# A ConvLSTM and bottleneck kernel: h stored and loaded in 128 lanes where it lay in 96

## The reference, cut to what matters

```
xr = transpose(x, (2, 0, 1, 3))                       # rows first
hs_f = scan(xr, w_f, b_f, reverse=False)              # h of 48 channels, a row at a time
hs_b = scan(xr, w_b, b_b, reverse=True)
feats = concatenate([hs_f, hs_b], axis=2)             # 96 channels
y = einsum('oc,bchw->bohw', w_proj, feats)            # 48 channels
y = gamma * normalised(y) + beta;  x1 = relu(y) + x
```

## Time and profile before

| | |
|---|---|
| median of 3 runs | 1834.93 us (1831.94 to 1840.61) |
| the profiled execution | 1834.02 us |
| its span, from the first to the last instruction | 1832.2 us |
| mean granted TensorE clock | 0.953 |
| busy share: PE, weight load, DVE, ACT, POOL | 90%, 67%, 77%, 70%, 3% |
| the DMA queue of SP, share of the 16 engines over the span | 40.1% |
| HBM read and written | 98.71 and 61.49 MB |

### The profile page before, as it was taken

How to read it: one execution, slowest core, us unless ns; L and a number is a source line. 1 busy time by engine, 2 the same in 40 slices (tenths; PEclk the granted TensorE clock), 3 DMA queues, 4 the chain that set the end, 5 groups by cost and what they waited for, 6 DMA issues and landing times. The chain is left out here.

```text
span 1832.2 us, 43864 instructions
## 1 busy us (share of the span) xinstructions
PE 1646.6 (90%) x16562; PEld 1236.4 (67%) x16562; DVE 1402.7 (77%) x2264; ACT 1276.9 (70%) x2347; POOL 57.9 (3%) x88
## 2 busy tenths in 40 slices
PE   5999999999999999999996662449999999999996
PEld 5999999999999999999994220137333333333332
DVE  4777777777777777777775447643999999999996
ACT  4888888888888888888885445401666666666663
POOL 2000000000000000000000000001000000000000
PEclk9999999999999999999998996655999999999998
DMA  4555455554555555455555998892122222222223
GB/s 118 137 138 143 131 146 136 141 140 132 144 135 145 137 136 143 133 147 136 139 143 125 246 246 164 203 306 67 23 44 44 47 47 49 46 44 45 44 44 50
DMA packets 82905, 219.04 MB, mean 120 GB/s; under 512 B 20792, under 2 KB 26828, under 8 KB 82380
## 3 DMA queue, kind: packets, MB, share of 16 engines
q1 hardware_dynamic: 74504, 193.89, 40.1%
q0 software_dynamic: 6144, 16.52, 6.3%
q10 hardware_dynamic: 2180, 7.57, 2.0%
HBM read 98.71 MB, written 61.49 MB: 87 GB/s over the span
## 5 line engine op out<-in xcount | busy, mean ns | idle before, releaser
L264 PE MATMUL gates<-state,w_high 64*128 64x384 f32 x4608 | 504.9, 337 | 0.0
L1374 DVE SCALAR_TENSOR_TENSOR acc<-h1d,wt,acc 128x768 f32<-128x768 f32 x480 | 483.3, 1017 | 25.0 <-ACT acc L1285 11.8
L264 PEld LDWEIGHTS gates<-state,w_high 64*128 64x128 f32 x4608 | 416.9, 185 | 0.0
L1152 PE MATMUL psd<-h1p,wt 64*64 64x384 f32 x3456 | 300.9, 487 | 11.3 <-ACT h2p L1317 11.3
L264 PE MATMUL gates<-state,w_low 64*128 64x384 f32 x2304 | 267.6, 337 | 0.0
L264 PE MATMUL gates<-x_both,w_high 64*128 64x384 f32 x2304 | 237.4, 338 | 18.8 <-DVE w_low L380 18.8
L1152 PEld LDWEIGHTS psd<-h1p,wt 64*64 64x64 f32 x3456 | 126.2, 132 | 186.8 <-issue 172.7
L264 PEld LDWEIGHTS gates<-x_both,w_high 64*128 64x128 f32 x2304 | 207.5, 186 | 18.7 <-issue 18.7
L317 ACT ACTIVATE sig_f<-gates 48x384 f32<-48x384 f32 x384 | 187.3, 488 | 37.2 <-PE gates L264 32.3
L264 PEld LDWEIGHTS gates<-state,w_low 64*128 64x128 f32 x2304 | 208.8, 185 | 0.0
L411 DVE TENSOR_TENSOR h_new<-sig_o,tanh_c 128x384 f32<-128x384 f32 x192 | 107.2, 558 | 122.3 <-ACT tanh_c L335 122.3
(11 more groups left out here) (141 smaller groups left out, 1619.5 us busy)
## 6 DMA issues: line engine op xcount, KB each, us to landing
x_taps<-x_both SPq DMA_DIRECT2D x192, 195.5 KB, 3.1
x_raw<-x_steps SPq DMA_DIRECT2D x192, 192.0 KB, 3.2
h_rows<-h_new SPq DMA_DIRECT2D x192, 144.0 KB, 2.3
h_in<-h_rows SPq DMA_DIRECT2D x48, 576.0 KB, 7.7
x_last<-x_both SPq DMA_DIRECT2D x192, 98.0 KB, 2.9
out<-y SPq DMA_DIRECT2D x4, 4032.0 KB, 37.6
out<-z POOLq DMA_DIRECT2D x48, 336.0 KB, 5.0
sig_o<-x_steps SPq DMA_DIRECT2D x190, 48.0 KB, 2.0
```

Of the source, the lines that this page charges most:

```text
L264: return nc.tensor.matmul(gates[p][d][:, m, 0:NH], w[own, n, m, :], moving[own], start=start, stop=stop)
L1152: mm = nc.tensor.matmul(psd[64 * m:64 * m + 64, i, 0:NH], wt[own, to:to + 64], h1[own, dy + 4 * m:dy + 4 * m + 4, dx:dx + W], start=(tap = ...
L1374: nc.vector.scalar_tensor_tensor(a, window(h1d[d % 2], tap), par(D_UNITS[s], TAP + tap), a, ALU.mult, ALU.add).then_inc(acc_done if tap == ...
```

## The change

`h_rows` gets all 128 lanes. A store copies the 64 lanes of a direction, with the 16 lanes of x beside the 48 of h. A load brings 128 lanes. In the projection the weights come in one DMA with 128 lanes, those of the lanes with x being zeros; no lane is left without data, so the five memsets, their semaphore and the waits for it are gone.

```diff
             def store_h(i, e):
                 for d in range(2):
                     two = i if d == 0 else i * -1 + (H // 2 - 1)
-                    sp.dma_start(h_rows[two, HC * d:HC * d + HC, e if d == 0 else 1 - e],
-                                 h_new[e][HI * d:HI * d + HC]).then_inc(h_stored[e], 16)
+                    own = slice(HI * d, HI * d + HI)
+                    sp.dma_start(h_rows[two, own, e if d == 0 else 1 - e], h_new[e][own]).then_inc(h_stored[e], 16)
...
-        wp_loaded, gaps_zero = sem("wp_loaded"), sem("gaps_zero")
+        wp_loaded = sem("wp_loaded")
...
-            sp.wait_ge(gaps_zero, 1)
-            for d in range(2):
-                sp.dma_start(wp[HC * d:HC * d + HC], w_proj[HI * d:HI * d + HC]).then_inc(wp_loaded, 16)
-
-            def body(i, first):
+            sp.dma_start(wp[:], w_proj).then_inc(wp_loaded, 16)
+
+            def body(i):
                 for n in range(BUFS):
-                    if first:
-
-                        sp.wait_ge(gaps_zero, n + 2)
                     r = TURN * i + ROWS * n

                     at_least(sp, row_summed, r - TURN + ROWS)
-                    sp.dma_start(h_in[n][0:2 * HC], h_rows[BUFS * i + n]).then_inc(h_loaded[n], 16)
+                    sp.dma_start(h_in[n][:], h_rows[BUFS * i + n]).then_inc(h_loaded[n], 16)
...
-            pe.wait_ge(wp_loaded, 32)
+            pe.wait_ge(wp_loaded, 16)
...
-            nc.vector.memset(wp[96:128], 0.0).then_inc(gaps_zero, 1)
-            for n in range(BUFS):
-                nc.vector.memset(h_in[n][96:128], 0.0).then_inc(gaps_zero, 1)
...
-    h_rows = nc.dram_tensor("h_rows", [H // 2, 2 * HC, 2, B, W], F32).ap()
+    h_rows = nc.dram_tensor("h_rows", [H // 2, P, 2, B, W], F32).ap()
```

More of the change, by code:

```diff
@@ L459, in _ @@
         def _(sp):
-            sp.wait_ge(gaps_zero, 1)
-            for d in range(2):
-                sp.dma_start(wp[HC * d:HC * d + HC], w_proj[HI * d:HI * d + HC]).then_inc(wp_loaded, 16)
-            def body(i, first):
+            sp.dma_start(wp[:], w_proj).then_inc(wp_loaded, 16)
+            def body(i):
                 for n in range(BUFS):
-                    if first:
-                        sp.wait_ge(gaps_zero, n + 2)
                     r = TURN * i + ROWS * n
                     at_least(sp, row_summed, r - TURN + ROWS)
-                    sp.dma_start(h_in[n][0:2 * HC], h_rows[BUFS * i + n]).then_inc(h_loaded[n], 16)
-            body(0, True)
+                    sp.dma_start(h_in[n][:], h_rows[BUFS * i + n]).then_inc(h_loaded[n], 16)
+            body(0)
             with sp.Fori(1, H // TURN) as i:
-                body(i, False)
+                body(i)
         @block.tensor
         def _(pe):
-            pe.wait_ge(wp_loaded, 32)
+            pe.wait_ge(wp_loaded, 16)
             def body(i, first):
```

## The result

The kernel after takes 1816.39 us (median, 1814.15 to 1818.11) beside 1834.41 us for the kernel before, a ratio of 0.990 with a 95% interval of 0.988 to 0.9925. That is 18.0 us less; the forecast was 15.8 us less, 1818.2 us. The profiled execution took 1815.6 us, its span 1813.8.

What follows compares the result with a forecast made beforehand. The prediction took DMA loads to bound the projection and PE the recurrence; -14.7 - 1.3 + 0.2 = -15.8 us from 1834.0 gave 1818.2 us, with a range of 1806 to 1834 us.

Steps and rivals of the forecast that it cites:

- The bound: Projection: one h_in transfer paces each pair of rows, 48 x 2.38 = 114 us; the recurrence is paced by PE.
- T: Projection: time of one pair's h_in load, 2.377 us a pair before, forecast 2.07 us with 128 lanes.
- Part 1: Projection loads: 128 lanes for 96, 786,432 bytes at 380 GB/s, 2.07 us a pair for 2.377: -14.7 us.
- my trend: Projection loads: packets shorten as lanes are added, 0.0365 us for 16 more, so 0.2585 us at 128 lanes.
- rival of the same pace per byte: Projection loads: a packet keeps its 0.398 us, 3.18 us a pair, slower at 1871.4 us; chance 0.11.
- rival of lanes 0 to 63: Projection loads: the first 64 lanes set the pace, 2.38 us a pair stays, 1832.9 us; chance 0.14.
- 408.7 GB/s of a stream of loads: Projection loads: a skill page's rate for 1 MiB transfers, an estimated 1.92 us a pair, stage some 22 us shorter.
- Part 2: Projection start: one wp load and no memset before the first h_in load, so it goes out earlier: -1.3 us.
- Part 3: Recurrence stores with 64 lanes for 48: recurrence at 0, share 0.52 to 0.56, last store's landing +0.2 us.

Runs made afterwards that it cites:

- the repeat: The kernel after itself, unchanged, timed and profiled once more beside two other kernels on one chip: 1814.54 us, ratio 0.991 to the kernel before.

## Why the prediction was right, point by point

- **The bound.** Right: the projection is bound by the DMA engines before and after, and its time is about T times 48. (I read 9 and 8 in slices 22 and 23 of the DMA row; it has 9 and 9.)
- **Part 1, T = 2.07 us and -14.7 us.** The sign holds, and that the loads pace the stage. The size was 3.8 us short in the first execution (18.5 us, 0.39 us off each of 47 periods) and 1.2 us short in the repeat (15.9 us). By the windows T is 2.00 us where I said 2.07. The step that does not hold is the path to T. I read a smooth trend, a packet that gets shorter as lanes are added, through 48, 96 and 112 lanes. There is none. The table has the loads of the same stage; its last column is the median time of a 6144-byte packet in the traces' packet records, 1010 to 1050 us:

| lanes | packets per engine | GB/s | T, us | median packet, us |
|---|---|---|---|---|
| 0 to 63 | 4 | 207 | 1.90 | 0.479 |
| 0 to 95 | 6 | 246 | 2.40 | 0.401 |
| 16 to 111 | 6 | 245 | 2.41 | 0.409 |
| 0 to 111 | 7 | 263 | 2.62 | 0.378 |
| 0 to 63 and 64 to 127 | 4 + 4 | 224 | 3.51 | 0.451 |
| 0 to 127 | 8 | 394 | 2.00 | 0.234 |
| 0, 2 ... 126 and 1, 3 ... 127 | 4 + 4 | 382 | 2.06 | 0.234 |
| 0, 2 ... 126 and 1, 5 ... 125 | 4 + 2 | 339 | 1.74 | 0.234 |

 With lanes spread over all 128 the packet takes 0.234 us, however many packets a load has, and 8 of them make the 1.87 us of most pairs; with other lanes it takes 0.38 to 0.48 us. The row of 112 lanes that carried my trend (333 GB/s) was a store with rows of 36,864 bytes; the load of 112 lanes makes 263. With its 0.374 us a packet the same working would have given 0.357 us at 128 lanes, T = 2.86 us, and a slower kernel. That my T is near the measured one is luck: the trend through the wrong row happened to point at the step between 112 and 128.
- **The rival of the same pace per byte** (0.398 us a packet, T = 3.18). By the rates it is near for 96 and 112 lanes (0.400 and 0.374 us) and fails at 128 (0.250 us).
- **The rival of lanes 0 to 63.** It put T at 2.38 us and is wrong by that, but half of it is true: with lanes 0 to 63 alone T is 1.90 us, so lanes 64 to 127 cost 0.1 us in a load of all 128. The reason I gave against it, that x_in gets only 223 GB/s with both halves, does not reach it, as x_in's halves are two transfers; two transfers by halves make 224 here too. The Trainium skill's page "SBUF — State Buffer", section "Door 1: The DMA port swizzle", lets the bandwidth go by how many of 16 ports the lanes reach, at 27.2 GB/s a port, with eight lanes to a port. Read as a limit of the fullest port, this makes an estimate of 1.81 us for 8 lanes in it, and 0.9 for each even or odd half. The runs are 5 to 14% above that at lanes 0 to 63, at 128 and at even and odd (1.90, 2.00 and 2.06 us), and it does not describe 96 and 112 lanes, which have 8 in the fullest port too and take 2.4 to 2.6.
 The Trainium skill's page "DMA: Bandwidth & Descriptors", section "The descriptor swizzle", says how a transfer of 128 lanes is dealt out: each engine writes the lanes of one port alone. If an engine gets 6 or 7 neighbouring lanes in a load of 96 or 112, its block straddles ports, and engines would meet there. This is a guess that fits the table; that it is the cause was not shown, as the profile does not give the lanes of an engine.
- **The 408.7 GB/s of a stream of loads**, from the Trainium skill's page "DMA: Bandwidth & Descriptors", section "iDMA fabric", was near: single pairs go at 786,432 / 1.88 = 418 GB/s, the mean is 394 (381 in the repeat).
- **Part 2, the start, -1.3 us.** Right: -1.19 us from wp load to first h_in load, and -0.3 us before it, as no memset of wp is waited for; 1.34 us with the memsets of the buffers put back.
- **Part 3, the stores.** The recurrence costs nothing: PE 450.00 of 450 us, share 0.56 as forecast. The last stores were forecast at +0.2 us and took about +0.6. The landing is 0.3 us of it (the median over all stores went from 2.3 to 2.7 us, where I said 2.5). The other 0.33 us is a term that I left out: SP needs 1.11 us to issue the two of 64 lanes and 0.78 for the two of 48. The +0.53 us before them is not the change's: in the timelines below the matmul groups from 23.09 us differ (0.73 us long before, 1.17 after), in instructions that the change does not touch. The granted clock is 1.00 in both there, so it does not tell why. In the repeat the last stores are issued at 984.64, as in the kernel before.

Timelines of PE at the start, before and after:

```profile
23.09 0.73 PE L264 MATMUL gates<-state,w_low 64*128 64x384 f32 x6
23.67 1.23 PE L264 MATMUL gates<-state,w_high 64*128 64x384 f32 x12
```
```profile
23.09 1.17 PE L265 MATMUL gates<-state,w_low 64*128 64x384 f32 x6
24.05 1.46 PE L265 MATMUL gates<-state,w_high 64*128 64x384 f32 x12
```

So -18.5 for the loads, -1.5 for the start and +0.6 for the last stores, with 0.5 and 0.4 us of scatter elsewhere, give the 18.4 us of span.

## What to carry to other kernels

When a stage is bound by loads, look at the rate under the full DMA share: the share was about 1.0 from 207 to 394 GB/s. Here, with 6144 bytes a lane and four loads in flight, it paid to load all 128 lanes though a quarter of the bytes was useless, and more to spread the 96 useful ones over all 128 by a step; 96 or 112 neighbouring lanes were slower than 128 in time, not only in rate. Try these forms where a load has fewer than 128 lanes. And take the price of a transfer from a row of its own form and direction, since a store with other rows gave the right answer here for a wrong reason.

## What the runs showed of the hardware that was not expected

- A load of 112 lanes (2.62 us) takes longer than one of 128 (2.00 us), with 6144 bytes a lane in both.
- Two transfers by even and odd lanes are as fast as one (382 GB/s; 394 and 380 in the two executions of one); two by halves are not (224).
- The packet of 6144 bytes takes 0.234 us in the median with lanes spread over all 128, and 0.38 to 0.48 us with 64, 96 or 112 neighbouring lanes.
- SP's issue of one DMA depends on the form (medians): 317 ns for 96 and 112 lanes, 333 for 128, 469 to 475 for loads of 64; 351 for the stores of 48 lanes and 504 for those of 64. In the kernel after it was hidden everywhere but at the last stores.
- Single pairs take 2.2 to 3.0 us where most take 1.88, some eight times in the projection of the first execution and a dozen in the repeat; the longest in the middle of the stage came with a 16 KB packet of instructions in the DMA engines.
